# Expert results of layer 0: stored in block order and fetched by index, instead of scattered to token order

## What is computed

```
x = x + attention_L(layernorm(x), context)      # 4 x 77 keys
x = x + ffn_L(layernorm(x))
```

```
scores = sigmoid(xf @ gate_w.T)
_, sel = top_k(scores + expert_bias, 2);  top_scores = scores[sel]
for each expert e:
    w_t = sum(where(sel == e, top_scores, 0))
    h   = square(relu((xf * w_t) @ wu.T))       # hidden 256
    out = out + h @ wd.T
```

## Time and profile before

| | |
|---|---|
| median of three runs | 874.91 us (869.89 to 875.44) |
| the profiled execution | 870.93 us |
| its span, first to last instruction | 869.2 us |
| mean granted TensorE clock | 0.939 of full speed |
| TensorE busy | 734.0 us, 84% |
| VectorE busy | 546.6 us, 63% |
| ScalarE busy | 504.0 us, 58% |
| GpSimd busy | 289.3 us, 33% |
| indirect sends L2145, all routed layers | 64, mean 971 ns |
| plain reads of `ys` (L2252), all routed layers | 12 of 256 KB, 3.4 us from issue to landing |

### The profile page before, as it was taken

One profiled execution on the slowest core, in us unless ns is written; L12 is line 12 of the kernel. 1 busy time (PEld: TensorE's weight loads), 2 busy tenths in 40 slices (PEclk: granted clock), 3 DMA queues, 4 the chain that ended last, 5 costly groups with the idle time before them and its releaser, 6 DMA issues.

```text
span 869.2 us, 16741 instructions
## 1 busy us (share of the span) xinstructions
PE 734.0 (84%) x5129; PEld 598.7 (69%) x5129; DVE 546.6 (63%) x1935; ACT 504.0 (58%) x1720; POOL 289.3 (33%) x345
## 2 busy tenths in 40 slices
PE   3878875768779898899999889989999998776597
PEld 1566654647666577777996677878778876666597
DVE  3668844646657788764546888784232066786575
ACT  2677754245546888764656555567544248563375
POOL 0420033244561445353451444432010024243355
PEclk9799998688999999999999999999999999797599
DMA  8897995113317110001315660000000050000121
GB/s 279 274 204 172 298 207 158 69 44 87 82 56 244 44 47 8 8 14 41 83 42 172 200 181 1 2 2 0 1 1 1 1 195 1 1 17 13 48 73 47
DMA packets 37735, 74.21 MB, mean 85 GB/s; under 512 B 7360, under 2 KB 26944, under 8 KB 33680
## 3 DMA queue, kind: packets, MB, share of 16 engines
q1 hardware_dynamic: 32304, 62.97, 26.2%
q0 software_dynamic: 4768, 9.91, 3.3%
q10 hardware_dynamic: 576, 0.27, 0.1%
HBM read 63.03 MB, written 37.67 MB: 116 GB/s over the span
## 4 chain that ended last, share of the span: by engine, by line
PE 53%; DVE 19%; ACT 9%; issue 9%; POOL 6%; another core or an unknown queue 2%; DMA 1%; SPq 0%; DVEq 0%; POOLq 0%; ACTq 0%
PE bank L1250 10%; PE bank L1142 6%; PE bank L1212 5%; PE bank L1222 5%; PE bank L1104 4%; PE bank L1118 4%; DVE s_xn L1432 3%; POOL out L2152 3%; PE bank L1050 3%; PE bank L1095 2%; POOL xs_L L2145 2%; PE bank L1202 2%; DVE s_total L1484 2%; ACT s_S L1942 2%
## 5 line engine op out<-in xcount | busy, mean ns | idle before, releaser
L2117 POOL TENSOR_TENSOR s_S<-s_S,s_inv 128x462 f32<-128x462 f32 (+2 forms) x123 | 100.5, 833 | 143.4 <-DVE s_inv L1487 141.8
L1118 PEld LDWEIGHTS bank<-s_ident,s_S 128*128 128x128 f32 (+2 forms) x560 | 69.4, 145 | 76.9 <-issue 36.0
L1118 PE MATMUL bank<-s_ident,s_S 128*128 128x128 f32 (+2 forms) x560 | 90.7, 284 | 27.2 <-POOL s_S L2117 9.0
L1977 ACT ACTIVATE s_PT<-bank 128x512 f32<-128x512 f32 (+2 forms) x160 | 80.3, 505 | 55.5 <-PE bank L1118 45.3
L1104 PE MATMUL bank<-s_A,s_xTq 128*128 128x462 f32 (+2 forms) x256 | 105.4, 509 | 4.5 <-ACT s_S L1963 1.5
L1142 PE MATMUL bank<-s_VW,s_PT 128*128 128x128 f32 (+2 forms) x800 | 100.9, 282 | 0.0
L2145 POOL DMA_INDIRECT xs_L<-s_xn,s_sli x64 | 62.1, 971 | 114.5 <-DVE s_sli L1591 74.5
L1142 PEld LDWEIGHTS bank<-s_VW,s_PT 128*128 128x128 f32 (+2 forms) x800 | 96.9, 198 | 0.0
L1942 ACT ACTIVATE s_S<-bank,s_peak 128x77 f32<-128x77 f32 x256 | 59.1, 359 | 13.3 <-DVE s_peak L1456 13.3
L1963 ACT ACTIVATE s_S<-bank,s_peak 128x77 f32<-128x77 f32 x192 | 60.8, 348 | 4.5 <-DVE s_peak L1473 4.3
L2019 ACT ACTIVATE s_hT<-bank,s_b1T 128x128 f32<-128x128 f32 x184 | 52.3, 370 | 18.4 <-PE bank L1222 9.3
(11 more groups left out here) (236 smaller groups left out, 1650.1 us busy)
## 6 DMA issues: line engine op xcount, KB each, us to landing
xs_L<-xs_L SPq DMA_DIRECT2D x24, 1122.0 KB, 28.0
s_xe<-xs_L SPq DMA_DIRECT2D x85, 66.0 KB
s_moe<-in_L_w SPq DMA_DIRECT2D x2, 2048.0 KB, 10.7
s_moe<-in_L_w SPq DMA_DIRECT2D x8, 512.0 KB, 7.6
s_yb<-ys_L SPq DMA_DIRECT2D x12, 256.0 KB, 3.4
s_A<-in_keys SPq DMA_DIRECT2D x4, 616.0 KB, 6.7
s_arena<-in_L_w SPq DMA_DIRECT2D x2, 1024.0 KB, 12.2
s_arena<-in_L_h SPq DMA_DIRECT2D x2, 1024.0 KB, 9.2
```

The costliest lines, as they stand in the source:

```text
L1118: w = turn(bank[b][0:m, P * (t - t0):P * (t - t0) + P], S[s][:, P * t:P * t + m], ident)
L1977: w = a(flat(PT[k][:, full[0]:full[-1] + 1, :]), b[:, P * (full[0] - t0):P * (full[-1] - t0) + P], ACT.Copy)
L2117: p.tensor_tensor(val, val, rep(inv[s][:, h0:h1], KEYS, 2), ALU.mult).then_inc(normed.up(L, i, k), 1)
```

## The change

The results of layer 0's experts are no longer scattered. They are stored as they come, block after block, by eleven plain DMAs on SP (`STORES`: nine of four blocks, one of two, one of one). Each token's two rows are then fetched by index, two indirect DMAs on GpSimd for each tile (`gather`), 32 in all. The index is the token's place in its expert's bucket, corrected by the expert's first block (`compact`, five VectorE instructions in step 12 of the expert stage). The weight is now applied when the rows are added to x (`comb`), one instruction for each tile and choice. So the rows carry no weight and no mark of the choice, VectorE makes no `sel`, `yi` and `yw` for layer 0, and it copies `xeT` in place of ScalarE. Layer 1's query groups become tile 0, tiles 1 to 3, and then fours as before. Its first two groups (tiles 0 to 3) are prepared in the passage, the other three inside the attention.

The plan, and the waits' class (`Transfers` gets a step, since two DMAs count on one semaphore):

```diff
+STORES = [*((j, j + 4) for j in range(0, 36, 4)), (36, 38), (38, 39)]
-Q_GROUPS = {0: [(0, 1), (1, 4), (4, 8), (8, 12), (12, 16)],
-            **{L: [(0, 4), (4, 8), (8, 12), (12, 16)] for L in (1, 2, 3)}}
+Q_GROUPS = {**{L: [(0, 1), (1, 4), (4, 8), (8, 12), (12, 16)] for L in (0, 1)},
+            **{L: [(0, 4), (4, 8), (8, 12), (12, 16)] for L in (2, 3)}}
...
     def backs(L, g):
+        if L == 0:
+            return [("gather", 0, i) for i in range(*tiles("q", 1, g))]
...
-        if L in (1, 2) and g == 1:
+        if L == 2 and g == 1:
             norm = norm[3:]
...
-        out += [("weigh", L, g, st) for st in range(3)] if L != 1 else [2]
+        out += [[("weigh", L, g, st) for st in range(2 + (L == 3))], [2]][L == 1]
...
-                if s == max(0, t0 - 5) and g > (L in (0, 3)):
+                if s == max(0, t0 - 5) and g > (L != 2):
                     side(f"before{g}", before(L, g))
...
+        if L == 1:
+            more = [p for p in norm_rows("q", 1, 1) if not isinstance(p, int)]
+            for piece in [*backs(0, 0), *backs(0, 1), *keys, *combs(0, 0), *norm, *vwt[:4], ("xt", "q", 1, 0),
+                          *vwt[4:8], *combs(0, 1), *more, *vwt[8:12], ("xt", "q", 1, 1), *vwt[12:]]:
+                put(*piece)
+            return
...
+            if L == 0:
+                for q, (j0, j1) in enumerate(STORES):
+                    if j1 == s - 2:
+                        put("store", q)
+                if s == 12:
+                    put("compact")
```

VectorE:

```diff
-                    v.tensor_copy(xn[:, tt, FIRST], ixf[:, 0, 0:n])
...
-                    v.tensor_copy(xn[:, tt, W0], wgt[:, 0, tt])
-                    v.tensor_tensor(ysf[:, 0, 0:n], wgt[:, 1, tt], wgt[:, 0, tt], ALU.subtract).then_inc(own.up(), 1)
-                    again()
-                    v.tensor_scalar(xn[:, tt, W1], ysf[:, 0, 0:n], 1.0 / 2048, None, ALU.mult).then_inc(weighed.up(0, g), 1)
...
+            elif kind == "compact":
+                picked = jt[0][:, 0:2 * NT, :]
+                dve.wait_ge(*block_expert.at(0))
+                v.tensor_reduce(ahead, windows(cs[0], 0, 8), AX, ALU.add).then_inc(own.up(), 1)
+                again()
+                v.scalar_tensor_tensor(ahead, ahead, float(P), ebase, ALU.mult, ALU.subtract).then_inc(own.up(), 1)
+                again()
+                v.tensor_tensor(picked, OH.rearrange("p c t e -> p (c t) e"), rep(ahead, 2 * NT, 1),
+                                ALU.mult).then_inc(own.up(), 1)
+                again()
+                v.tensor_reduce(ixall, picked, AX, ALU.add).then_inc(own.up(), 1)
+                again()
+                v.tensor_tensor(compact, slf, ixall.rearrange("p (c t) -> p c t", c=2), ALU.add).then_inc(indexed.up(), 1)
...
-                if L == 1:
+                if L != 3:
                     dve.wait_ge(*x_sum.at(L, j))
...
                     v.tensor_copy(xeT[j % 2], bank[b][:, 0:P]).then_inc(x_back.up(L, j), 1)
...
-                if L == 0:
-                    v.tensor_scalar(sel[j % 2], row[:, FIRST:FIRST + 1], jf[0][:, j:j + 1], 2048.0, ALU.not_equal,
-                                    ALU.mult).then_inc(own.up(), 1)
-                    again()
-                    v.scalar_tensor_tensor(yi[k], sel[j % 2], row[:, TOK:TOK + 1], dump[:, k:k + 1], ALU.add, ALU.min)
-                    v.tensor_scalar(yw[k], sel[j % 2], row[:, W1:W1 + 1], row[:, W0:W0 + 1], ALU.mult,
-                                    ALU.add).then_inc(tags.up(L, j), 1)
...
                 if j >= YO:
-                    dve.wait_ge(*returned.at(L, j - YO))
+                    dve.wait_ge(*(returned.at(L, j - YO) if L else yo_left(j - YO)))
...
-                    v.tensor_scalar(yo[j % YO], src, yw[k], None, ALU.mult).then_inc(y_made.up(L, j), 1)
+                    v.tensor_copy(yo[j % YO], src).then_inc(y_made.up(L, j), 1)
...
             elif kind == "comb":
                 L, g, c = at
+                if L == 0:
+                    t0, t1 = tiles("q", 1, g)
+                    dve.wait_ge(*weighed.at(0, last_of(0)))
+                    if c:
+                        dve.wait_ge(*own.at(after["comb"]))
+                    for i in range(t0, t1):
+                        dve.wait_ge(*gathered.at(0, i))
+                        w = v.scalar_tensor_tensor(x[:, i, :], yb[c][:, i % 4, :], wgt[:, c, i:i + 1], x[:, i, :],
+                                                   ALU.mult, ALU.add)
```

GpSimd and SP:

```diff
-                if L != 1:
+                if L == 3:
                     pool.wait_ge(*weighed.at(L, g))
-                if L == 3:
...
-            elif kind == "D":
+            elif kind == "gather":
+                L, i = at
+                pool.wait_ge(*indexed.at())
+                for q in range(len(STORES)):
+                    pool.wait_ge(*stored.at(q))
+                if i >= 4:
+                    pool.wait_ge(*comb.at(0, asked_of(1, i - 4)))
+                if gathered.before(L, i)[1]:
+                    pool.wait_ge(*gathered.before(L, i))
+                for c in range(2):
+                    p.indirect_dma_start(yb[c][:, i % 4, :], None, ys[0],
+                                         bass.IndirectOffsetOnAxis(ap=compact[:, c, i:i + 1], axis=0)
+                                         ).then_inc(gathered.up(L, i), 16)
+            elif kind == "D" and at[0] != 0:
...
+            elif kind == "store":
+                q0, = at
+                j0, j1 = STORES[q0]
+                sp.wait_ge(*y_made.at(0, j1 - 1))
+                if stored.before(q0)[1]:
+                    sp.wait_ge(*stored.before(q0))
+                q.dma_start(ys[0][P * j0:P * j1, :].rearrange("(t p) d -> p t d", p=P),
+                            yo4[j0 // 4 % 3][:, j0 % 4:j0 % 4 + j1 - j0, :]).then_inc(stored.up(q0), 16)
```

More of the change, by code:

```diff
@@ L153, in ends @@
             if n:
-                yield s, 16 * n
+                yield s, self.step * n
 class Engine:
@@ L687, in body @@
     here = put("here", [P, 8])
-    slf = put("slf", [P, 2, 4])
+    slf = put("slf", [P, 2, NT])
+    compact = put("compact", [P, 2, NT], I32)
+    ahead = put("ahead", [P, 8])
+    ixall = put("ixall", [P, 2 * NT])
     sli = put("sli", [P, 2, NT], I32)
@@ L701, in body @@
     yb = [put(f"yb{i}", [P, 4, P]) for i in range(2)]
-    sel = [put(f"sel{i}", [P, 1]) for i in range(2)]
     yi = [put(f"yi{i}", [P, 1], I32) for i in range(YO)]
-    yws = put("yw", [P, YO])
-    yw = [yws[:, i:i + 1] for i in range(YO)]
     xq = put("xq", [P, 4, P])
@@ L730, in body @@
     xeT = [put(f"xeT{i}", [P, P]) for i in range(2)]
-    yo = [*(yb[k][:, i, :] for k in (0, 1) for i in range(4)), *(put(f"yo{i}", [P, P]) for i in range(8, YO))]
+    yo4 = [*yb, put("yo8", [P, 4, P])]
+    yo = [y[:, i, :] for y in yo4 for i in range(4)]
     Vbd = [put(f"Vbd{i}", [P, C0], at=at_m + 4 * C0 * i) for i in range(2)]
@@ L907, in body @@
     block_in = Transfers(ctx, nc, "block_in", ((L, j) for L in ROUTED for j in range(BLOCKS[L])), XE)
-    returned = Transfers(ctx, nc, "returned", events("D"), YO)
+    stored = Transfers(ctx, nc, "stored", events("store"), 2)
+    returned = Transfers(ctx, nc, "returned", (a for a in events("D") if a[0] != 0), YO)
+    gathered = Transfers(ctx, nc, "gathered", events("gather"), 2, 2 * 16)
     cleared = Transfers(ctx, nc, "cleared", ((L, e) for L in ROUTED for e in range(NE)), 8)
@@ L933, in x_turned, with yo_left @@
     def x_turned(L, j):
-        return (x_back if L == 1 else x_copied).at(L, j)
+        return (x_copied if L == 3 else x_back).at(L, j)
+    def yo_left(j):
+        return stored.at(next(q for q, (j0, j1) in enumerate(STORES) if j0 <= j < j1))
     def asked(g, j, b):
@@ L952, in x_before @@
             return x_ffn.at(i)
[L953 removed]
+        return comb.at(L - 1, asked_of(L, i))
     def last_score(L):
@@ L1586, in vector_program @@
                     dve.wait_ge(*own.at(after["route"]))
-                    v.tensor_reduce(slf[:, 0:topk, 0:n], both[:, 0:topk, 0:n, :], AX, ALU.add).then_inc(own.up(), 1)
+                    v.tensor_reduce(slf[:, 0:topk, tt], both[:, 0:topk, 0:n, :], AX, ALU.add).then_inc(own.up(), 1)
                     after["route"] = own.n
@@ L1903, in scalar_program @@
                 u, L, g = at
+                t0, t1 = tiles(u, L, g)
                 act.wait_ge(*xt_sum.at(u, L, g))
@@ L1918, in scalar_program @@
                         act.wait_ge(*gates.at(*r_of[use["gate", ("r", L, g)] - 2][1:]))
-                t0, t1 = tiles(u, L, g)
-                a(flat(dst)[:, 0:P * (t1 - t0)], bank[bank_t[piece]][:, 0:P * (t1 - t0)],
+                a(flat(dst[:, 0:t1 - t0, :]), bank[bank_t[piece]][:, 0:P * (t1 - t0)],
                   ACT.Copy).then_inc(xt_made.up(u, L, g), 1)
@@ L1989, in scalar_program @@
                   scale=-1.0).then_inc(sig_exp.up(L, g), 1)
-            elif kind == "X" and at[0] != 1:
+            elif kind == "X" and at[0] == 3:
                 L, j = at
-                if L == 3:
```

(11 more changed lines are left out.)

80 lines of the change are left out of this document (39 added, 41 removed).

## The result

In 20 runs each, the changed kernel takes 876.07 us at the median (872.21 to 880.92) and the kernel before 873.65 (868.61 to 879.14). The ratio is 1.0038, with a 95% interval of 1.002 to 1.0057: slower by 3 us, within the 1% that was called no change, and not the gain of 4 us that was forecast. The profiled execution of the changed kernel, 872.21 us, is its fastest run; it lies 1.3 us above the one of before.

What follows compares the result with a forecast made beforehand. TensorE, busy 84%, was taken as nearest to a bound. Terms -19.7 + 1.0 - 0.5 + 2.5 + 10 + 2.7 = -4.0 us took 870.93 to 866.9; predicted 868 us, likeliest case 860 to 876, 8 in 10 852 to 886.

Steps and rivals of the forecast that it cites:

- Part (a): Layer 0's expert stage: eleven SP stores replace 39 GpSimd scatters, gaining 19.7 us, with 1 us lost to compact.
- Part (b): Layer 0's routing: four small VectorE instructions fewer in each of five groups, 0.5 us gained.
- (c): Passage to layer 1: gathers delay first scores from 17.8 to 21.8 us after the last product; net 2.5 us lost.
- (d): Layer 1's attention: 24 gathers delay GpSimd's divisions, 10 us lost: 3 for the first group, 3.5 for each other.
- The landings: Passage: the gathers were to land 1.7 us after the eighth's issue ended.
- The 1.5 us given back: Layer 1's first attention steps: half the normalisation of tiles 4 to 7 and its transposes leave, returning 1.5 us.
- (e): Layer 1's attention: four wide adds become 24 weighted ones, 8.2 against 2.7 us on VectorE; 2.7 us lost.
- The waits for L2117: Layer 1's attention: TensorE's waits for GpSimd's divisions, 11.0 us before, were to exceed 20 us.
- The first (gaps take the gathers): Layer 1's attention: GpSimd's idle gaps absorb the gathers, gathers and adds costing 3 us, not 12.7; 858 us, chance 30%.
- the third (the scatters are innocent): First expert stage: its gaps are not from scatters, so the stores gain nothing or 3 us; 885 us, chance 12%.
- The second: Layer 1's attention: three gather bursts freeze the other engines, 6.4 us each; 881 us, chance 17%.
- The fourth: Layer 1's attention: weighted adds wait 0.7 us each for GpSimd's divisions, 17 us at most; 879 us, chance 8%.

Runs made afterwards that it cites:

- e1: Kernel before with layer 0's 39 expert scatters as plain DMAs on SP, nothing else changed: 856.62 us, 0.981 of the kernel before.
- e5: The changed kernel again, no edit, on a chip of the second kind: 857.36 us beside 836.79 for the kernel before, ratio 1.0242.
- e6: Kernel before with only the eleven stores in place of the 39 scatters: 829.59 us beside 836.79, ratio 0.991.
- e9: The kernel before again, no edit, profiled on a chip of the second kind: 845.02 us in the profiled execution.
- e2: Changed kernel with SP's weight loads held until the gathers of tiles 0 to 3 landed: 870.93 us, 0.998 of the kernel before.
- e14: Changed kernel with all gathers as plain reads on SP and all adds unweighted, one per group and choice: 841.36 us, 1.005 of the kernel before.
- e3: Changed kernel with the 24 gathers inside layer 1's attention as plain reads on SP: 868.66 us, 0.994 of the kernel before.
- e4: Changed kernel with each group's eight weighted adds in layer 1's attention as two unweighted ones: 872.65 us, 1.000 of the kernel before.
- e15: Changed kernel with layer 1's order and groups as in the kernel before, gathers and weighted adds kept: 883.96 us, 1.010 of the kernel before.
- e16: Changed kernel with layer 1's old order, weight loads held to the last gather, ring of four semaphores: 876.56 us, 1.0025 of the kernel before.
- e8: Changed kernel with weight loads held until the last gather landed and a ring of four semaphores for gathers: 853.54 us, 1.019 of the kernel before.

## Why the prediction was wrong

The forecast was a gain of 4 us and the measurement a loss of 3; the time itself lay in the range. The parts, on the kind of chip that the forecast was made from:

**The stage was right.** Part (a) forecast 19.7 us less 1 for compact, and the stage gave 21.4. The reading of the earlier trace rows was right too: e1 removes only the scatters and the gaps go. It was incomplete. e5, e6 and e9 show that there are two things in it: the scatters' own rate of 1.26 us a block against the 1.00 that TensorE needs, on both kinds of chip, worth 7 us of the kernel's time in e6, and a hold-up of the other engines, on some chips only. The first was in the earlier trace rows. That the second is not on every chip could not be told from the rows of one; that not every burst is held up could, since the same trace has the two bursts of six. Nothing in the text asked for either. Part (b), 0.5 us, is too small to be checked.

**The step that failed is (c), the passage,** with what it said of the first steps of attention. It forecast first scores at 21.8 us after the last product, and they came at 26.4. It gave back 1.5 us for work that leaves the attention, and tile 4's scores came another 7.3 us late instead (24.5 against 17.2 us after the first). It was to be 2.5 us, with 3 for the first group in (d); it was 15.9. Four things were missed:
- The landings. They were put at 1.7 us; the chain shows 6.30 and 3.99. SP's weight loads used to stand behind the reads in the same queue. Once the reads are on GpSimd, nothing holds the loads back. The step named the queue that the stores go to, and not what follows them there (e2: 5 us in the passage, 0.6% in time, of which its profile shows only 1.7 us over passage and attention together). The ring of two was in the diff and was not costed.
- The group of tiles 4 to 7. Its adds and statistics move from the passage, where TensorE's products covered VectorE (TensorE busy 16 of 17 us), into the attention's start. Its adds had a price, its statistics had none. e14 against e6 gives the order 11 us, with neither gathers nor weighted adds, and 9 of them build up over tiles 4 to 7.
- The 1.5 us given back. The row instructions and transposes of this group were to leave the attention and did not: VectorE makes 12 row instructions for layer 1's queries there before and 12 after. This half stayed, and the other half joined it.
- The clock. TensorE's idle 9 us of the passage and the thin start are followed by windows at 0.60 and 0.50 of full speed. The sum had no term for it. The kernel before has one such window at 0.74 between 266 and 302 us, the others at 0.98 or more. How much of the 15.9 the clock holds was not separated.

**Parts (d) and (e)** forecast 10 + 2.7. The 3 of the first group aside, that is 9.7 from tile 4 on, where 8.8 was lost. That they are close is luck in part: behind tile 4's scores 5.2 us belong to the order (e14 against e6), 2.5 to the adds, and none that shows to the gathers, to which (d) had given 7. By their times e3 and e4 give gathers and adds in the attention 8 and 4 us, near the 10 and 2.7, but no profile shows the 8 in the two later groups. The waits for L2117 were to pass 20 us and came to 18.0.

**The rivals.** The first (gaps take the gathers) and the third (the scatters are innocent) fell. The second fell as well: gathers back to back did not hold up the engines, on either kind of chip (passage and attention of the changed kernel take 174.7 us on the first and 173.2 on the second); beside the eight in this window of the changed kernel, on a chip of the first kind, TensorE is busy 7.40, VectorE 6.89 and ScalarE 5.74 of 9.8 us:

```profile
262.90:272.70 9.80, 7.40 (x17) 3.15 (x16) 6.89 (x16) 5.74 (x31) 7.62 (x9) 0.90 0.19 48
```

The fourth had the right mechanism at a smaller price: 3 us was lost in the 24 adds, not 12, and it was lost in four of them. The Trainium skill's rule (SBUF — State Buffer, "Who interferes with whom") fits the 1.66 us beside a division, and the two adds that began 0.16 us before a division and took the usual 0.31; most adds did not meet one.

## What to carry to other kernels

When a transfer is taken off a queue, look at what stood behind it in that queue: its order was a brake. When the order of pieces changes, cost every piece of the moved group, by what covered it in the old place and what is free in the new one. And before a hold-up that no semaphore explains is built on, look for the places in the same trace where the supposed cause is present and nothing is held up, and time the pair on more than one chip.

## What was not expected of the hardware

- On the chips of the result, of e1 to e4 and of e15 and e16, the other engines were held up beside back-to-back indirect scatters from GpSimd, for 16 us of layer 0's attention (two bursts of eight, changed kernel) and 16 us of the first expert stage (66.8 against 51.0); on those of e5 to e14 the same program ran through. Two bursts of six at the same rate held up nothing on the first kind. What differs, between the chips and between the bursts, stays open.
- Indirect gathers at the same rate, 1.26 us from start to start and up to eight in a row, stopped nothing on either.
- A gather of 128 rows landed in about 2.5 us with the weight loads held (e2, e8) and in 6.3 us beside 4864 KB of them at 393 GB/s.
